# Output projection of a linear-attention block: three bf16 passes over split halves of o, or one fp32 pass over o itself

## What is computed

```
q = (x @ Wq).reshape(b, s, h, dh); k = (x @ Wk)...; v = (x @ Wv)...     # 64 heads of 64, dim 128
q = relu(q) * SCALE;  k = relu(k)
kv  = einsum('bsid,bsjd->bsdj', k, v)          # per token; equals relu(q) . (relu(k)^T v)
out = einsum('bsid,bsdj->bsij', q, kv)
out = out / (einsum('bsid,bsd->bsi', q, k.sum(axis=2)) + 1e-6)
x1  = layernorm(x + out.reshape(b, s, 4096) @ Wo + bo)
h   = silu(fp4(x1) @ fp4(w_gate).T) * (fp4(x1) @ fp4(w_up).T)
y   = layernorm(x1 + fp4(h) @ fp4(w_down).T)
```

## Time and profile before

| | |
|---|---|
| time, median of 3 runs | 2371.66 us (2352.8 to 2376.55) |
| the profiled execution's own time | 2365.52 us |
| its span, first to last instruction | 2363.7 us, mean granted PE clock 0.969 |
| PE busy | 2079.3 us, 88% |
| DVE busy | 1937.1 us, 82% |
| POOL busy | 1676.8 us, 71% |
| ACT busy | 1489.2 us, 63% |
| DMA, share of 16 engines | 59.3% |

### The profile page before, as it was taken

The page is one execution under the profiler, slowest core; times in us unless marked ns, Lnnn a source line. Parts: engine busy times, 40 slices in busy tenths (PEclk is TensorE's granted clock), DMA queues, the critical chain, the costliest instruction groups (busy, mean ns, idle before and its releaser), DMA issues.

```text
span 2363.7 us, 88235 instructions
## 1 busy us (share of the span) xinstructions
PE 2079.3 (88%) x37963; PEld 1977.0 (84%) x37963; DVE 1937.1 (82%) x3933; ACT 1489.2 (63%) x2634; POOL 1676.8 (71%) x2064
## 2 busy tenths in 40 slices
PE   3799999999898999999989999899889989989975
PEld 3788898888888888888888888889888888888864
DVE  7678888888888888888888888888888888888874
ACT  4566666666666666666666666666666666666651
POOL 3577787777677777777767767678667767767773
PEclk8899999999999999999999999999999999999986
DMA  6366656656655755665665665666665655655651
GB/s 186 83 132 148 135 129 136 147 125 130 148 121 123 152 126 120 149 134 115 147 135 113 147 129 118 148 129 129 138 132 116 147 126 121 148 128 120 147 119 39
DMA packets 523212, 308.29 MB, mean 130 GB/s; under 512 B 275590, under 2 KB 497734, under 8 KB 522310
## 3 DMA queue, kind: packets, MB, share of 16 engines
q1 hardware_dynamic: 522822, 302.65, 59.3%
HBM read 17.38 MB, written 4.19 MB: 9 GB/s over the span
## 4 chain that ended last, share of the span: by engine, by line
PE 46%; POOL 18%; ACT 16%; DVE 13%; issue 6%; DMA 1%; DVEq 0%; ACTq 0%; SPq 0%; POOLq 0%
PE ps L360 11%; ACT q_bd L564 11%; PE ps L362 10%; PE ps L361 10%; PE ps L407 10%; POOL o_st L1066 8%; POOL q_nat L1056 8%; DVE q L766 4%; DVE o L790 3%; ACT q_nat L597 2%; PE ps L444 1%; PE ps L459 1%; ACT hqT L571 1%; DVE v_st L749 1%; PE ps L426 1%
## 5 line engine op out<-in xcount | busy, mean ns | idle before, releaser
L1066 POOL TENSOR_TENSOR o_st<-o,o_st 128x256 bf16<-128x256 f32 x1024 | 662.8, 677 | 75.5 <-ACT o_st L623 73.7
L1056 POOL TENSOR_TENSOR q_nat<-q,q_nat 128x512 bf16<-128x512 f32 x512 | 591.1, 1176 | 60.3 <-ACT q_nat L597 60.1
L360 PE MATMUL ps<-v_st,q_bd 128*128 128x66 bf16 x4096 | 462.9, 200 | 139.5 <-ACT q_bd L564 73.4
L360 PEld LDWEIGHTS ps<-v_st,q_bd 128*128 128x128 bf16 x4096 | 421.3, 115 | 169.9 <-DVE o L790 85.4
L623 ACT CAST o_st<-o 128x256 bf16<-128x256 f32 x1024 | 356.6, 404 | 310.2 <-DVE o L790 308.1
L361 PE MATMUL ps<-v_st,q_bd 128*128 128x66 bf16 x4096 | 459.4, 199 | 0.0
L362 PE MATMUL ps<-v_st,q_bd 128*128 128x66 bf16 x4096 | 458.3, 198 | 0.0
L361 PEld LDWEIGHTS ps<-v_st,q_bd 128*128 128x128 bf16 x4096 | 421.7, 117 | 0.3 <-issue 0.2
L362 PEld LDWEIGHTS ps<-v_st,q_bd 128*128 128x128 bf16 x4096 | 420.1, 116 | 0.0
L597 ACT CAST q_nat<-q 128x512 bf16<-128x512 f32 x512 | 292.0, 617 | 179.0 <-DVE q L766 178.8
L749 DVE TENSOR_TENSOR v_st<-ps,v_st 128x1024 bf16<-128x1024 f32 x256 | 312.4, 1222 | 106.4 <-ACT v_st L540 99.4
(11 more groups left out here) (125 smaller groups left out, 5411.9 us busy)
## 6 DMA issues: line engine op xcount, KB each, us to landing
q_bd<-q_nat SPq DMA_DIRECT2D x256, 256.0 KB, 4.1
swap<-v_st SPq DMA_DIRECT2D x64, 576.0 KB, 6.4
v_st<-v_st SPq DMA_DIRECT2D x64, 576.0 KB, 5.3
v_st<-swap SPq DMA_DIRECT2D x64, 576.0 KB, 5.5
swap<-o_st SPq DMA_DIRECT2D x64, 512.0 KB, 4.3
o_st<-o_st SPq DMA_DIRECT2D x64, 512.0 KB, 8.4
o_st<-swap SPq DMA_DIRECT2D x64, 512.0 KB, 6.0
x_in<-in_L_attn_x SPq DMA_DIRECT2D x64, 64.0 KB, 5.6
```

What stands on the lines that cost most here:

```text
L360: nc.tensor.matmul(dst, lhs(0), rhs(0), start=True, stop=False)
L1056: last = nc.gpsimd.tensor_tensor(qnat[:, 1, a, :, e, :], src[:, a], qnat[:, 0, a, :, e, :], ALU.subtract)
L1066: last = nc.gpsimd.tensor_tensor(lo[:, :, a], src[:, a], hi[:, :, a], ALU.subtract)
```

## The change

w_o stays fp32 as it is loaded, `o_st` is one fp32 buffer of the same bytes, and DVE writes it directly: each `scale_o` is two instructions of 128x256, one per block half, with no ring. `o_hi` on ACT and `o_lo` on POOL are gone, and so is the splitting of w_o. `wo_part` issues one fp32 matmul for each j, where there were three in bf16. `y` moves to ACT as y = r2*rs2 + nb, with nb = -mean*rs2 that POOL makes in two more one-column instructions. The order changes: ACT does q_stay(0,1) ahead of hq_copy; DVE does mean_1 ahead of v_lo(0), and x_round and k_fold(2) ahead of norm_o(0); POOL does h_back after the next iteration's rstd_1, and q_stay waits for it; SP issues the two q moves of line 290 ahead of the first o move; at the start, the splitting of w_q comes after v_hi(2) on ACT and v_lo(2) on DVE. The lines that matter:

```diff
-        w_o = sb("w_o", [P, 2, HALF * DIM], BF16)
+        w_o = sb("w_o", [P, HALF * DIM])
...
-        o_st = [sb(f"o_st{i}", [P, 2 * 2 * S * HALF], BF16) for i in range(2)]
+        o_st = [sb(f"o_st{i}", [P, 2 * S * HALF]) for i in range(2)]
         swap = sb("swap", [P, 2 * S * VS], BF16)
-        o32 = sb("o32", [P, OR, G * DH])
...
-        ost = [o[:, :].rearrange("p (l f b s e) -> p l f b s e", l=2, f=NE, b=2, e=EB) for o in o_st]
-        omat = [o[:, :].rearrange("p (l f t e) -> p l f t e", l=2, f=NE, e=EB) for o in o_st]
+        ost = [o[:, :].rearrange("p (f b s e) -> p b s f e", f=NE, b=2, e=EB) for o in o_st]
+        omat = [o[:, :].rearrange("p (f t e) -> p f t e", f=NE, e=EB) for o in o_st]
...
-                if t.mid:
-                    groups, om = ((t.m + 1) * NG), [(t.m * 48 + 16 * i) for i in range(3)]
-                    sp.wait_ge(s_ohi, groups)
-                    sp.wait_ge(s_olo, groups)
-                    move(o4[t.par], osw, s_oswap, om[0], 0)
                 if t.attend:
                     sp.wait_ge(s_qlo, (t.n * NC))
                     q_move(1, 0)
                     q_move(1, 1)
+                if t.mid:
+                    groups, om = ((t.m + 1) * NG), [(t.m * 48 + 16 * i) for i in range(3)]
+                    sp.wait_ge(s_read["out"], groups)
+                    move(o4[t.par], osw, s_oswap, om[0], 0)
...
-                        pe.wait_ge(s_wlo["o"], 1)
+                        pe.wait_ge(s_wload["o"], 32)
                         pe.wait_ge(s_ks, t.n + 1)
                 j0, j1 = WO_PARTS[i]
                 for j in range(j0, j1):
-                    for k, (lo, lw) in enumerate(((0, 0), (0, 1), (1, 0))):
-                        last = nc.tensor.matmul(Y, omat[t.par][:, lo, j // EB, :, j % EB], womat[:, lw, j, :],
-                                                start=(j == 0 and k == 0), stop=(j == HALF - 1 and k == 2))
+                    last = nc.tensor.matmul(Y, omat[t.par][:, j // EB, :, j % EB], womat[:, j, :],
+                                            start=(j == 0), stop=(j == HALF - 1))
...
-            def o_hi(t, g):
-                if not t.attend:
-                    return
-                if g == 0 and t.is_(2):
-                    act.wait_ge(s_wlo["o"], 1)
-                if g == 0 and t.back:
-                    act.wait_ge(s_y, t.b + 1)
-                act.wait_ge(s_read["out"], t.o * NG + g + 1)
-                src = o32[:, g % OR, :].rearrange("p (s b f e) -> p b f s e", b=2, f=NE, e=EB)
-                for a in range(2):
-                    last = nc.scalar.copy(ost[1 - t.par][:, 0, :, a, g * G:(g + 1) * G, :], src[:, a])
-                last.then_inc(s_ohi, 1)
+            def y(t):
+                if t.end:
+                    act.wait_ge(s_store, 16 * (t.e + 1))
+                    act.wait_ge(s_nb, t.e + 1)
+                    nc.scalar.activation(y_out[:, :], r2[:, :], ACT.Identity, bias=nb[:, 0:1],
+                                         scale=rs2[:, 0:1]).then_inc(s_yo, 1)
...
                 v_hi(t, 2)
+                if t.is_(0):
+                    weight_hi("q")
                 v_hi(t, 3)
                 x_hi(t)
                 k_first(t)
-                if t.is_(0):
-                    weight_o_hi()
                 q_stay(t, 1, 0)
+                q_stay(t, 0, 1)
                 hq_copy(t)
-                q_stay(t, 0, 1)
                 q_stay(t, 0, 0)
...
-                o_hi(t, 0)
-                o_hi(t, 1)
+                y(t)
                 q_hi(t, 1)
-                o_hi(t, 2)
-                o_hi(t, 3)
                 q_hi(t, 2)
-                o_hi(t, 4)
                 h_step(t)
-                o_hi(t, 5)
                 q_hi(t, 3)
-                o_hi(t, 6)
-                o_hi(t, 7)
...
-            for k in "vkq":
+            def weight_lo(k):
...
+            weight_lo("v")
+            weight_lo("k")
...
-                i = t.o * NG + g + 1
-                dve.wait_ge(s_rec, i)
-                if not (t.is_(1) and g < OR):
-                    dve.wait_ge(s_olo, i - OR)
-                nc.vector.tensor_tensor(
-                    o32[:, g % OR, :].rearrange("p (s b e) -> p s b e", b=2, e=HALF),
-                    slot_cols(("out", g))[:, :, 0:PW].rearrange("p s (b e) -> p s b e", b=2)[:, :, :, 0:HALF],
-                    rec[:, g % NR, :].unsqueeze(2).unsqueeze(3).to_broadcast([P, G, 2, HALF]),
-                    ALU.mult).then_inc(s_read["out"], 1)
+                if g == 0 and t.is_(1):
+                    dve.wait_ge(s_ffnw, 2)
+                if g == 0 and t.back:
+                    dve.wait_ge(s_y, t.b + 1)
+                dve.wait_ge(s_rec, t.o * NG + g + 1)
+                src = slot_cols(("out", g))[:, :, 0:PW].rearrange("p s (b e) -> p b s e", b=2)
+                for a in range(2):
+                    last = nc.vector.tensor_tensor(
+                        ost[1 - t.par][:, a, g * G:(g + 1) * G],
+                        src[:, a, :, 0:HALF].rearrange("p s (f e) -> p s f e", f=NE),
+                        rec[:, g % NR, :].unsqueeze(2).unsqueeze(3).to_broadcast([P, G, NE, EB]), ALU.mult)
+                last.then_inc(s_read["out"], 1)
...
-            def y(t):
-                if t.end:
-                    dve.wait_ge(s_rs2, t.e + 1)
-                    dve.wait_ge(s_store, 16 * (t.e + 1))
-                    nc.vector.scalar_tensor_tensor(out=y_out[:, :], in0=r2[:, :], scalar=mv2[:, 0:1],
-                                                   in1=rs2[:, 0:1].to_broadcast([T, DIM]), op0=ALU.subtract,
-                                                   op1=ALU.mult).then_inc(s_yo, 1)
...
                 before_mean_1(t)
+                mean_1(t)
                 v_lo(t, 0)
-                mean_1(t)
                 v_lo(t, 1)
                 v_lo(t, 2)
+                if t.is_(0):
+                    weight_lo("q")
                 x_one(t)
...
                 k_fold(t, 1)
+                x_round(t)
+                k_fold(t, 2)
                 norm_o(t, 0)
-                k_fold(t, 2)
-                x_round(t)
+                x_grid(t)
                 recip(t, 0, 1)
-                x_grid(t)
                 stats_2(t)
...
-            pool.wait_ge(s_whi["o"], 1)
-            nc.gpsimd.tensor_tensor(w_o[:, 1, :], stage["o"], w_o[:, 0, :], ALU.subtract).then_inc(s_wlo["o"], 1)
+            pool.wait_ge(s_tree, 3)
...
-            def o_lo(t, g):
-                if not t.attend:
-                    return
-                pool.wait_ge(s_ohi, t.o * NG + g + 1)
-                src = o32[:, g % OR, :].rearrange("p (s b f e) -> p b f s e", b=2, f=NE, e=EB)
-                hi, lo = (ost[1 - t.par][:, l, :, :, g * G:(g + 1) * G, :] for l in range(2))
-                for a in range(2):
-                    last = nc.gpsimd.tensor_tensor(lo[:, :, a], src[:, a], hi[:, :, a], ALU.subtract)
-                last.then_inc(s_olo, 1)
...
+                    nc.gpsimd.tensor_tensor(nm[:, :], mv2[:, 0:1], consts[:, 5:6], ALU.mult).then_inc(s_nm, 1)
+                    pool.wait_ge(s_rs2, t.e + 1)
+                    pool.wait_ge(s_nm, t.e + 1)
+                    nc.gpsimd.tensor_tensor(nb[:, :], nm[:, :], rs2[:, :], ALU.mult).then_inc(s_nb, 1)
...
-                    pool.wait_ge(s_rs1, t.b + 1)
                     pool.wait_ge(s_x1, t.b + 1)
+                if t.end:
+                    pool.wait_ge(s_hq, t.e + 1)
...
                 rstd_1(t)
+                h_back(t)
                 q_stay(t)
                 x_back(t)
                 rstd_2(t)
                 q_lo(t, 0)
-                o_lo(t, 0)
-                o_lo(t, 1)
                 q_lo(t, 1)
-                o_lo(t, 2)
-                o_lo(t, 3)
+                x_bias(t)
                 q_lo(t, 2)
-                o_lo(t, 4)
-                o_lo(t, 5)
-                x_bias(t)
-                o_lo(t, 6)
-                h_back(t)
-                o_lo(t, 7)
                 q_lo(t, 3)
```

More of the change, by code:

```diff
@@ L56 @@
 NK = S // SB
-OR = 2
 EB = 4
@@ L155, in attention_ffn @@
         warm = sb("warm", [P, 1])
-        consts = sb("consts", [P, 5])
+        consts = sb("consts", [P, 6])
         r1, x1, xm, xq = (sb(v, [T, DIM]) for v in ("r1", "x1", "xm", "xq"))
@@ L166, in attention_ffn @@
         mv1, mv2 = sb("mv1", [T, 2]), sb("mv2", [T, 2])
-        ve1, rs1, ve2, rs2 = (sb(v, [T, 1]) for v in ("ve1", "rs1", "ve2", "rs2"))
+        small = sb("small", [T, 6])
+        ve1, rs1, ve2, rs2, nm, nb = (small[:, i:i + 1] for i in range(6))
         ps = ctx.enter_context(nc.psum_tensor("ps", [P, 8, 512], F32))
@@ L215, in attention_ffn @@
         s_nrm, s_rec = sem("s_nrm"), sem("s_rec")
-        s_ohi, s_olo, s_oswap = sem("s_ohi"), sem("s_olo"), sem("s_oswap")
+        s_oswap = sem("s_oswap")
         (s_xres, s_xb, s_y, s_r1, s_st1, s_agg1, s_ve1, s_rs1, s_x1, s_xmax, s_xsc, s_xrs, s_xn, s_xm, s_xk, s_xt, s_xs,
@@ L221, in attention_ffn @@
```

(20 more changed lines are left out.)

12 lines of the change are left out of this document (6 added, 6 removed).

## The result

The changed kernel takes 2834.2 us (median of 4 runs, 2834.0 to 2837.3) against 2373.8 us for the kernel before (4 runs, 2352.8 to 2376.6): a ratio of 1.196, with a 95% interval from 1.190 to 1.202. It is slower by 20%, where I forecast 2337 us and a gain of 1.5%. The profiled execution has a span of 2832.3 us.

A forecast was written before the change was run, and what follows sets the result against it. PE's order with its gaps was taken as the loop's clock. Per tile +1.75 - 0.55 - 0.6 = +0.6, +37 us for 61 tiles, then -48, -8, -2.5, -4 and -8 (clock): in all -34, forecast 2337 us, range 2300 to 2410.

The forecast's parts named there:

- the part on the output projection: Projection on PE: 32 fp32 matmuls as 64 records of 0.112 take 7.2 us against 5.4, +1.75 us per tile.
- the bf16 rows' 15 ns: Projection's weight load: the step costs 15 ns on 64 records, +1.0 us per tile; as a rival about 2400, chance 0.13.
- the fp32 load is slow with its step: Rival on the projection's weight load: each load takes twice as long, +8.9 us per tile, 2790 us; chance 0.14.
- Nothing hides it.: Projection on PE: its +1.75 us shows in full, as PE has no idle between the parts.
- The first attention group, -0.55: Around the first attention group: q_bd's wait moves to `down`, and `k_sum` starts earlier, -0.55 us per tile.
- scale_o, -0.6: Scaling of o on DVE: no wait for o_lo and a shorter h_scale let PE's out 4 and 5 start earlier, -0.6 us per tile.
- y, -48: y moved to ACT: 19 or 20 tiles with a long y each lose 2.4 us, -48 us in all.
- Start and tail: Ends of the run: folds at the start -8 us, first attention tile -2.5, tail -4.
- The clock: Granted PE clock: low stretches cost 21 us at most; with PE's gaps shorter, -8 us.

The follow-up runs named there:

- steps_bf16: The kernel before with the projection's bf16 weights read at steps of 1, 2, 4, 8 and 16 elements in its five parts, wrong values; 2388.7 us.
- swap_roles: The changed kernel with the projection's matmul operands exchanged: w_o loaded as weights, o streamed at its 16-byte step; 2809.4 us, ratio 1.189.
- order_y: The kernel before with y on ScalarE and the mended order, bf16 halves and three-matmul projection kept; 2293.2 us, ratio 0.971.
- hq_first: eb2 with hq_copy put back ahead of q_stay(0, 1) on ScalarE; 2364.3 us, ratio 0.999.
- y_act: The kernel before with only y moved to ScalarE and its two small instructions on GpSimd; 2318.6 us, ratio 0.982.
- eb2: The changed kernel with EB = 2 for 4, so o's columns for one j stand 8 bytes apart; 2366.9 us, ratio 1.0056 to the kernel before.

## Why the prediction was wrong, step by step

**The step that failed** is in the part on the output projection: "I take the lower value, the nearest fp32 row", 0.112 a record, with the bf16 rows' 15 ns as the upper end. It is a term of the sum that was mis-sized: +1.75 us per tile was forecast and +9.7 measured (5.44 to 15.15). The records are 0.233 apart. The rival "the fp32 load is slow with its step" named the mechanism and gave 2790 us with a record of 0.22; I gave it a chance of 0.14, because a bf16 load with the step loses only 15 ns. That was the wrong row to scale from. The bf16 step was 8 bytes and not 16, so the two rows said nothing of a step of 16 bytes, and in steps_bf16 a bf16 load at 16 bytes is 33 ns longer. The range ended at 2410 because the bound was taken from those rows. No row showed an fp32 read with a step, and the fp32 load was so long that the prediction itself said it might set the 0.112 already; the upper bound that fits this is the rival's doubled load.

The rival had the mechanism only on the load; swap_roles shows that the stream pays alike.

**"Nothing hides it."** Right. The projection's whole growth came out in the period, as PE had no idle time there.

**The first attention group, -0.55.** Right, and a little less in size. The wait of `k_sum` (0.46 in a tile) is gone after, and in order_y; the q_bd wait moved to `down` as 1.08; hq_first shows that it only moved. From y_act to order_y a tile falls by 0.42.

**scale_o, -0.6.** Right in kind and about in size. The instruction of 128x256 takes 413 ns, from a row of 417, and h_scale fell from 537 to 168 ns in the mean. The wait for the scaled o stays in order_y (0.7 a tile) and is 0.02 after.

**y, -48.** Right in kind, and 20 long tiles were counted rightly (19 or 20); that y_act gives 48.3 is partly luck, as told under that run: what I left out on either side cancels.

**Start and tail.** The fold at the start waits 1.5 us and not 8.6, and the first `k_sum` comes at 42.9 us where it came at 52.0: -9.1 for -8. The first attention tile is 6.6 us shorter (34.29 to 27.65) for -2.5, and the one ahead of it 2.0. Behind the last `k_sum` the span is 18.8 us longer with three projections in it, 29 us, so about 10 went there for -4. The same reckoning for eb2, which has the same order, gives about 6, and in order_y the stretch is 3.5 us longer than before. No run tests the tail alone, and its term stays open.

**The clock.** The mean granted clock of the span is 0.989 after and 0.969 before, and 0.982 in order_y, 0.988 in eb2. It went the way forecast; how much of the time it gave no run shows, as none changes it alone.

**The sum again.** With 9.7 for 1.75 in 61 tiles the forecast of 2337 becomes 2823; with three projections in the tail and what start and tail gave beyond the forecast it is about 2838, against 2834 measured. No term but that one is needed to explain the miss.

**What the gain would have come from.** Had the record been 0.112, the kernel would be like eb2 or a little better (7.2 for 7.77 us is 35 us less, so 2332 us as an estimate, 1% under the 2355 of the kernel before beside it), against order_y's 2293. At each of the three layouts the single fp32 pass is dearer than the three bf16 passes (15.15, 7.77 and 7.38 us per tile against 5.4), as the prediction's +1.75 had it. Of the gains per tile only that of `scale_o`, 0.7 of waits and 0.2 in the attention, needs the undivided o, and it is smaller than the 2.0 that the pass costs more at best; at the start the fold of 8.5 us, which order_y still has, needs it too. The other gains do without it.
